# Rounding the experts' gate and up weights: four chunks in each of two passes, or one chunk per pair of groups

## What is computed

```
x = layernorm(x + mamba(x))                      # conv, selective scan, gate, projection
x = layernorm(x + retention(x, ctx, ctx))        # q from x; k, v from ctx; xpos; decay mask; (q k^T * mask) v
x = layernorm(x + ffn(x))
# ffn: shared(x) + sum over the 2 best of 8 experts, weight * down_e(silu(gate_e x) * (up_e x))
# router: sigmoid(x @ router_w.T + bias), top 2, scores normalised to sum 1
```

## Time and profile before

| | us |
|---|---|
| three runs, median (lowest to highest) | 1889.92 (1889.55 to 1892.51) |
| profiled execution, span from the first to the last instruction | 1883.3 |
| TensorE busy in that span | 1717.4 (91%) |
| VectorE busy | 1182.4 (63%) |
| ScalarE busy | 802.5 (43%) |
| GpSimd busy | 719.7 (38%) |
| passes 0 to 14, from 605.75 to 1127.0 | 521.25 |

### The profile page before, as it was taken

One profiled execution on the slowest core, in us unless ns is written; L12 is line 12 of the kernel. 1 busy time (PEld: TensorE's weight loads), 2 busy tenths in 40 slices (PEclk: granted clock), 3 DMA queues, 4 the chain that ended last, 5 costly groups with the idle time before them and its releaser, 6 DMA issues.

```text
span 1883.3 us, 35442 instructions
## 1 busy us (share of the span) xinstructions
PE 1717.4 (91%) x9524; PEld 1437.6 (76%) x9525; DVE 1182.4 (63%) x2682; ACT 802.5 (43%) x1491; POOL 719.7 (38%) x625
## 2 busy tenths in 40 slices
PE   6999996999966899999999997999999999999980
PEld 4666655888854778888888885888888888888870
DVE  6777766888844666667666667555555555555546
ACT  5677767777721432232322324333333333333326
POOL 1011105888841343443544535323333333333333
PEclk9999997999986989999999998999999999999995
DMA  4444455777824332212222116333333333333329
GB/s 138 172 173 172 162 203 169 235 248 256 268 79 148 125 111 73 91 69 79 80 80 91 69 56 218 55 57 54 55 57 52 57 55 54 57 55 55 57 43 357
DMA packets 137705, 220.64 MB, mean 117 GB/s; under 512 B 40544, under 2 KB 110368, under 8 KB 129328
## 3 DMA queue, kind: packets, MB, share of 16 engines
q1 hardware_dynamic: 112064, 184.44, 29.9%
q0 software_dynamic: 25584, 35.54, 10.8%
HBM read 122.79 MB, written 97.12 MB: 117 GB/s over the span
## 4 chain that ended last, share of the span: by engine, by line
PE 47%; DMA 7%; POOL 6%; issue 5%; DVE 3%; ACT 2%; POOLq 0%; SPq 0%; DVEq 0%; ACTq 0%
PE back_ps L2486 17%; PE back_ps L2506 8%; PE back_ps L2388 5%; DMA acc<-back_y,back_token 5%; POOL back_turned_qk L1719 4%; PE back_ps L2374 3%; PE back_ps L2365 3%; PE back_ps L2495 3%; POOL sorted L1707 2%; PE back_ps L2319 2%; ACT back_out L1896 2%; PE back_ps L2327 2%; PE back_ps L2474 1%; PE back_ps L2284 1%; PE back_ps L2272 1%
## 5 line engine op out<-in xcount | busy, mean ns | idle before, releaser
L2486 PE MATMUL back_ps<-back_w_gu,back_xe_T 128*128 x1620 | 413.0, 404 | 2.2 <-DVE back_xe_T L2222 2.2
L1750 POOL DMA_INDIRECT acc<-back_y,back_token x135 | 209.0, 1548 | 462.2 <-DVE back_y L2241 367.9
L2486 PEld LDWEIGHTS back_ps<-back_w_gu,back_xe_T 128*128 128x128 f32 x1620 | 297.7, 189 | 62.0 <-issue 3.1
L2506 PE MATMUL back_ps<-back_w_down,back_he_T 128*128 x1620 | 225.5, 288 | 1.5 <-DVE back_he_T L2234 1.5
L2506 PEld LDWEIGHTS back_ps<-back_w_down,back_he_T 128*128 128x128 f32 x1620 | 200.9, 189 | 1.8 <-issue 1.7
L1179 PE MATMUL front_ps<-front_xn_T,front_w_in_parts 128*128 128x512 f32 x768 | 187.5, 400 | 5.1 <-issue 3.3
L1707 POOL DMA_INDIRECT sorted<-back_x,back_slot x128 | 136.0, 1062 | 134.8 <-DVE back_slot L2046 100.7
L1010 DVE SCALAR_TENSOR_TENSOR front_conv<-front_ps,front_conv_wb,front_conv 128x508 f32<-128x508 f32 (+2 forms) x192 | 141.3, 742 | 63.8 <-ACT front_conv L842 59.3
L1179 PEld LDWEIGHTS front_ps<-front_xn_T,front_w_in_parts 128*128 128x128 f32 x768 | 143.9, 191 | 48.8 <-issue 18.5
L2230 DVE TENSOR_TENSOR back_h<-back_h,back_ps 128x512 f32<-128x512 f32 x135 | 92.9, 688 | 117.5 <-PE back_ps L2486 117.5
L1890 ACT ACTIVATE back_he_T<-back_ps 128x512 fp32r<-128x512 f32 x135 | 80.7, 598 | 200.3 <-PE back_ps L2495 200.3
(11 more groups left out here) (230 smaller groups left out, 3036.2 us busy)
## 6 DMA issues: line engine op xcount, KB each, us to landing
back_xe<-sorted SPq DMA_DIRECT2D x135, 136.0 KB, 2.5
gate_T<-front_gate_T SPq DMA_DIRECT2D x16, 1024.0 KB, 4.7
xc_T<-front_xc_T SPq DMA_DIRECT2D x16, 1024.0 KB, 5.9
front_xc_in<-xc_T SPq DMA_DIRECT2D x16, 1024.0 KB, 5.3
front_gate_in<-gate_T SPq DMA_DIRECT2D x16, 1024.0 KB, 6.4
front_x_rows<-in_x SPq DMA_DIRECT2D x16, 512.0 KB, 5.5
front_c_rep<-c_parts SPq DMA_DIRECT2D x128, 64.0 KB, 4.4
front_rows_in<-in_x SPq DMA_DIRECT2D x16, 512.0 KB, 7.3
```

The lines of the kernel that those rows point to most:

```text
L1750: pool.indirect_dma_start(out=d["acc"][:, :], out_offset=bass.IndirectOffsetOnAxis(ap=token[:, r:r + 1], axis=0), in_=y[:, r % 2], in_offs ...
L2486: op = nc.tensor.matmul(dst[:, r % 2], xe_T[:, x_part, k], w_gu[:, bass.ds(e, 1), m, w_part, k], start=(n == 0), stop=(n == len(PASSES) - 1))
L2506: op = nc.tensor.matmul(ps_y[:, 0:D_MODEL], he_T[:, h_part, k], w_down[:, bass.ds(e, 1), w_part, k], start=(n == 0), stop=(n == len(DOWN_P ...
```

## The change

The same 16 chunks are rounded by the same two instructions each. Chunk 0 to 6 are now rounded one in each odd pass from 1 to 13, chunk 7 in pass 14, and 8 to 15 in pass 15 as before. Chunks 0 to 7 all pass through slot 1 of the raw buffer; chunks 8 and 9 are loaded in pass 0 into the other two slots and stay there until pass 15; chunk 10 is loaded at the end of pass 14. The gate and up weights lie in one tensor in memory so that the chunk's number can be a register. The diff, cut:

```diff
-        CHUNKS = [(e, m) for e in range(EXPERTS) for m in range(2)]
+        CHUNKS = EXPERTS * 2
+        EARLY = PAIRS - 1
+        w_chunk = w_gu.rearrange("p e m w k f -> p (e m) w (k f)")
+        def chunk_raw(c):
+            return 1 if not isinstance(c, int) or c < EARLY else c % 3
+        def chunk_loads(c):
+            if not isinstance(c, int):
+                return 16 * c + 16
+            return 16 * (1 + sum(chunk_raw(b) == chunk_raw(c) for b in range(c)))
@@ sync
             def load_chunks(*chunks):
                 for c in chunks:
-                    if c >= 3:
+                    if c >= EARLY + 3:
                         sp.wait_ge(chunk_ready, c - 2)
                     load_chunk(c)
@@ sync, step
-                if first:
+                if is_at(expert and expert[0], 0):
                     sp.wait_ge(w_ready, len(SPLIT))
-                    load_chunks(0, 1, 2)
+                    load_chunk(0)
+                    load_chunks(EARLY + 1, EARLY + 2)
...
-                        if first:
-                            load_chunks(3, 4)
-                        if second:
-                            load_chunks(7, 8)
...
                         store_base(g)
-                    if first:
-                        load_chunks(5, 6)
-                    if second:
-                        load_chunks(9, 10)
+                    if not is_at(g, GROUPS - 1) and expert[1]:
+                        sp.wait_ge(chunk_ready, (g - 1) // 2 + 1)
+                        load_chunk((g - 1) // 2 + 1)
+                    if is_at(g, GROUPS - 2):
+                        load_chunks(EARLY + 3)
@@ scalar, step, behind round_c and ahead of the copy of the logits
-                if is_at(expert and g, 0):
-                    chunk_high(0)
-                    chunk_high(1)
-                if is_at(expert and g, 1):
-                    chunk_high(4)
-                    chunk_high(5)
+                if expert and attention and u:
+                    chunk_high((g - 1) // 2)
+                if is_at(expert and g, GROUPS - 2):
+                    chunk_high(EARLY)
@@ scalar, end of the step
-                if is_at(expert and g, 0):
-                    chunk_high(2)
-                    chunk_high(3)
-                if is_at(expert and g, 1):
-                    chunk_high(6)
-                    chunk_high(7)
@@ vector, step, behind decay_scores and ahead of hidden(g, 2)
-                if is_at(expert and g, 0):
-                    chunk_low(0)
-                    chunk_low(1)
-                if is_at(expert and g, 1):
-                    chunk_low(4)
-                    chunk_low(5)
+                if expert and attention and u:
+                    chunk_low((g - 1) // 2)
+                if is_at(expert and g, GROUPS - 2):
+                    chunk_low(EARLY)
@@ vector, end of the step
-                if is_at(expert and g, 0):
-                    chunk_low(2)
-                    chunk_low(3)
-                if is_at(expert and g, 1):
-                    chunk_low(6)
-                    chunk_low(7)
```

More of the change, by code:

```diff
@@ L1587, in load_chunk @@
             def load_chunk(c):
-                e, m = CHUNKS[c]
-                sp.dma_start(raw[:, c % 3], d[("gate_w", "up_w")[m]][e].rearrange("p k f -> p (k f)")
-                             ).then_inc(raw_loaded[c % 3], 16)
+                of = d["gate_up_w"].rearrange("c p k f -> c p (k f)")
+                sp.dma_start(raw[:, chunk_raw(c)].unsqueeze(1), of[bass.ds(c, 1)].rearrange("c p f -> p c f")
+                             ).then_inc(raw_loaded[chunk_raw(c)], 16)
             sp.dma_start(ident, d["consts"][:, const_cols("ident")]).then_inc(ident_loaded, 16)
@@ L1629, in step @@
             def step(attention, expert):
-                first = is_at(expert and expert[0], 0)
-                second = is_at(expert and expert[0], 1)
-                if first:
+                if is_at(expert and expert[0], 0):
                     sp.wait_ge(w_ready, len(SPLIT))
-                    load_chunks(0, 1, 2)
+                    load_chunk(0)
+                    load_chunks(EARLY + 1, EARLY + 2)
                 if attention:
@@ L1776, in chunk_high @@
             def chunk_high(c):
[L1777 to L1779 removed]
+                act.wait_ge(raw_loaded[chunk_raw(c)], chunk_loads(c))
+                nc.scalar.activation(w_chunk[:, bass.ds(c, 1), 0], raw[:, chunk_raw(c)].unsqueeze(1),
                                      ACT.Copy).then_inc(chunk_high_ready, 1)
@@ L1911, in chunk_low @@
             def chunk_low(c):
-                e, m = CHUNKS[c]
                 dve.wait_ge(chunk_high_ready, c + 1)
-                nc.vector.tensor_tensor(w_gu[:, e, m, 1].rearrange("p k f -> p (k f)"), raw[:, c % 3],
-                                        w_gu[:, e, m, 0].bitcast(F32).rearrange("p k f -> p (k f)"),
-                                        ALU.subtract).then_inc(chunk_ready, 1)
+                nc.vector.tensor_tensor(w_chunk[:, bass.ds(c, 1), 1], raw[:, chunk_raw(c)].unsqueeze(1),
+                                        w_chunk[:, bass.ds(c, 1), 0].bitcast(F32), ALU.subtract
+                                        ).then_inc(chunk_ready, 1)
             def w_down_low(e):
@@ L2479, in up @@
                 if is_at(i, 0):
-                    pe.wait_ge(chunk_ready, len(CHUNKS))
+                    pe.wait_ge(chunk_ready, CHUNKS)
                 if not early(i):
@@ L2530, in launch_args @@
         "shared_down": chunks(a["L0_ffn_shared_down"].T),
-        **{n: np.stack([chunks(w) for w in a["L0_ffn_" + n]]) for n in ("gate_w", "up_w", "down_w")},
+        "gate_up_w": np.stack([chunks(w) for pair in zip(a["L0_ffn_gate_w"], a["L0_ffn_up_w"]) for w in pair]),
+        "down_w": np.stack([chunks(w) for w in a["L0_ffn_down_w"]]),
         "A_log": chunks(a["L0_attn_A_log"]), "D_skip": chunks(a["L0_attn_D_skip"])[:, :, 0].copy(),
```

3 lines of the change are left out of this document (removed).

## The result

The kernel after takes **1873.45 us**, the median of five runs (1871.64 to 1878.53); the kernel before, run beside it, 1889.55 (1882.31 to 1892.51). The ratio is 0.9931, 95% interval 0.9917 to 0.9946: a gain of 10 to 16 us.

The account below looks back on a forecast made before the run. TensorE was taken to bound the passes, at 33.83 us each from 4 to 13. Gains of 12.42 less costs of 1.5 and 0.4 gave 10.5 us off the 1883.3 span, plus 6.6 around it: 1879.4 us, range 1876.8 to 1884.2.

Parts of the forecast that it names:

- What bounds the kernel, and where the change pays: TensorE bounds the passes; removing chunk loads and roundings from passes 0, 1 and 2 gains 12.42 us.
- rival (B): Passes 1 and 2 are slow as first runs of their code, so nothing is gained: 1890; 0.08 including near-total partial latenesses.
- through the same late c_raw: Pass 2 lost 3.76 us because its context rows were loaded behind chunks 9 and 10; all of it removed.
- One rounding on ScalarE in each odd pass: Passes 1 to 13, between c_T and the logits copy: TensorE waits 0.55 us, costing 0.2 us a pass, 1.5 in all.
- the cover: Odd passes: TensorE's existing 0.32 us stand for GpSimd ahead of the scores hides part of the 0.55 us logits wait.
- Rival (C): The odd passes pay in full, 0.6 us each: 1882; counted within the forecast's own bounds, chance 0.82.
- One rounding on VectorE: Odd passes, behind the decayed scores: 1.22 us fits into 2.04 us of idle time, cost 0.
- One load on SP: End of odd passes, ahead of the next c_raw: c_raw still lands 1.7 us early, cost 0; far bound 1.2 in all.
- The estimate by the Trainium skill's limit: Even passes: at about 358 GB/s plus fixed 2 us a transfer, c_raw lands at 764.9, 0.3 us before wanted.
- The last pass: Chunk 10, loaded behind the last base store, lands late; ScalarE waits about 2 us, cost 0.4 us, bounds 0 to 1.3.
- The sum against the base: Whole kernel: 10.5 us off the profiled span 1883.3 gives about 1872.8; adding the unchanged 6.6 us gives 1879.4.
- pass 3's 0.34: Pass 3's 0.34 us over the later passes holds no chunk and stays; the bounds allow it gained or not.

Follow-up runs that it names:

- a_again: The kernel after, unchanged, run and profiled once more: 1875.86 us, ratio 0.9927 to the kernel before.
- b_again: The kernel before, unchanged, run and profiled once more: 1889.96 us, ratio 1.0.
- b_light: The kernel before with the loads of chunks 11 to 15 cut from 512 KB to 4 KB each: 1884.05 us, ratio 0.9988.
- b_context_first: The kernel before with chunks 5 and 6 loaded behind c_raw in pass 1, not ahead of it: 1883.73 us, ratio 0.9979 to before.

## Why the prediction was wrong

- *What bounds the kernel, and where the change pays*: right. Passes 0, 1 and 2 gave 1.0, 6.95 and 3.81 us (forecast 1.32, 7.34, 3.76), the waits by name are gone, and rival (B) is out. That pass 2 lost its time "through the same late c_raw" was right for about two thirds of it: by the two kernels with moved loads 0.7 us is the wait, 1.75 the clock behind it, and 1.3 VectorE's two roundings. In pass 0, where c_raw now stands behind three chunk loads, it can still be late: in a_again ScalarE waited 2.95 us for it, TensorE 0.75 for the logits.
- *One rounding on ScalarE in each odd pass*: the forecast wait of 0.55 us came (0.45), its price of 1.5 us in all did not. The failing step is the cover, taken as the 0.32 us in the bracket of the earlier trace rows; by the starts of the neighbouring groups it is about 0.5, and 0.52 was needed. Rival (C) is out.
- *One rounding on VectorE*: 0, right; no new wait on VectorE appeared in the odd passes.
- *One load on SP*: 0, right. In the three profiles of the kernel after ScalarE never waits for c_raw from pass 1 on. The step reckoned 1.7 us of room, the added loads say about 1.5. The estimate by the Trainium skill's limit ("DMA: Bandwidth & Descriptors", Specifications), by which the prediction had 0.3 us of room, is further off than that; its fixed 2 us are given in that page for transfers that GpSimd issues, and these loads are issued by SP.
- *The last pass*: chunk 10 is late by about what was reckoned (wait of 2.56 us, forecast about 2), the price of 0.4 us cannot be seen: taking the wait away gained nothing that the runs show, and the stretch varies by more than its size in both kernels.
- *The sum against the base* is the step that put the time outside the range: "what lies around the span (6.6 us to the median of the three runs, 1889.92) stays". No setting of the other terms reaches the measured time, since with every cost at 0 and pass 3's 0.34 gained they end at 1877.2. The 6.6 us are not what lies around the span: every run of both kernels that lists time and span has 1.65 to 1.8 us between them (1876.15 and 1874.4 for the profiled execution of after). So the profiled execution of before took about 1885.05 us by estimate, a short one among runs of 1882.3 to 1894.8, and the other 4.9 us were spread. With b_again, whose profiled run took 1890.05, these 5 us can be placed: 3.0 to the first tile, 1.0 in passes 4 to 13, 0.9 ahead of the opening step. The median of before itself was no outlier (1889.55, 1889.61 and 1889.54 in three batches, 1886.5 in the last); what the step lacked is a term for the spread, about 5 us each way, in a range that had terms for every cost. With 1.7 in place of 6.6 the forecast would have been 1874.5, and that this is near 1873.45 would have been luck: the three profiled executions of after have spans of 1874.4, 1875.9 and 1873.4 us against the forecast 1872.8.

Together: the costs of 1.9 us that were not paid, and a base that a single profile does not fix. The 1 to 2 us that would be needed to get from the 11.8 us of passes 0 to 3 to the 13.0 and 13.8 us of gain that the ratios of the first two batches give are inside their intervals, and are absent in the third (11.3); no run shows a place for them.

No kernel tried here beats the kernel after.

## What to carry to other kernels

Before a bulk load is put on a queue, look at what is issued behind it and when that is wanted: here four chunk loads in the wrong place cost some 8 us, and loads of the same size one at a time, each with about 1.5 us of room behind it, cost nothing. Read a slack from the starts of neighbouring groups in a pass with the wait and one without it, not from the idle bracket alone. And before a forecast is tied to a single profiled execution, ask where that execution stands among the runs: time less span is small and fixed, so anything more is spread and belongs into the range.

## What the runs showed of the hardware

- Waits of nearly one length were followed by different clocks: 1.99 us in pass 2 of before by 0.64 over 4 us and 1.85 us in b_light by 0.66, but 1.83 us in b_context_first by 1.00 throughout. Passes 2 of before and b_context_first are 1.75 us apart.
- At the turn of the loop ScalarE stands 0.6 to 1.35 us between two roundings in some turns and not in others, with the same code, for something that the profile does not name; TensorE pays 0.2 to 0.35 us for it. In pass 15 the same kind of idle time reached 7.8 us on ScalarE.
- A load of 512 KB more ahead of another on SP's queue moved the start of the work that waited for that other by 2.0 us (from one added load to two).
